# Expert stage of a routed feed-forward layer: row buffers released after the transposes, outputs two tiles to a bank, empty slots skipped in the adds

## The reference

```
x = layernorm(x + power_attention(x))            # 4 x 1024 tokens of 256 values
scores = softmax(x @ gate_w.T)                   # 64 experts
topk_w, topk_idx = top_k(scores, 6)              # 6 experts for each of the 4096 tokens
buf[e, slot] = x[token]                          # 64 x 768 slots; what is over 768 is dropped
g, u = buf @ w_gate[e].T, buf @ w_up[e].T        # 256 -> 176
eo = (silu(g) * u) @ w_down[e].T                 # 176 -> 256
y[token] += eo[e, slot] * weight(token, e)       # scatter-add back to the tokens
x = layernorm(x + y + shared_expert(x))
```

## Time and profile before

| | us |
|---|---|
| median of 3 runs (lowest, highest) | 2573.97 (2572.37, 2574.27) |
| the profiled execution, its own time | 2557.7 |
| its span in the profile | 2555.9 |
| busy in the span: PE / DVE / ACT / POOL | 2312.3 / 1397.8 / 1248.9 / 1578.3 |

### The profile page before, as it was taken

The page is one execution under the profiler, slowest core; times in us unless marked ns, Lnnn a source line. Parts: engine busy times, 40 slices in busy tenths (PEclk is TensorE's granted clock), DMA queues, the critical chain, the costliest instruction groups (busy, mean ns, idle before and its releaser), DMA issues.

```text
span 2555.9 us, 34620 instructions
## 1 busy us (share of the span) xinstructions
PE 2312.3 (90%) x11876; PEld 1793.6 (70%) x11880; DVE 1397.8 (55%) x2813; ACT 1248.9 (49%) x2302; POOL 1578.3 (62%) x1421
## 2 busy tenths in 40 slices
PE   5999999999999899999999999998797999989981
PEld 4777776776767677776667777666685887778871
DVE  2444444445564454557445455745666766656664
ACT  3444444444434344343444443434234777767764
POOL 2566555544578654457855445784074888788885
PEclk8999999999999999999999999999798999999996
DMA  3766741122123112111411211224355999889987
GB/s 125 302 238 261 279 157 63 54 63 64 40 64 119 54 52 87 40 40 69 138 31 53 88 40 38 71 76 146 119 188 163 216 212 202 193 197 213 210 165 230
DMA packets 162663, 329.68 MB, mean 129 GB/s; under 512 B 17552, under 2 KB 98192, under 8 KB 162480
## 3 DMA queue, kind: packets, MB, share of 16 engines
q1 hardware_dynamic: 114144, 262.01, 30.4%
q0 software_dynamic: 48192, 65.04, 14.0%
q10 hardware_dynamic: 144, 0.33, 0.0%
HBM read 172.21 MB, written 155.11 MB: 128 GB/s over the span
## 4 chain that ended last, share of the span: by engine, by line
PE 61%; POOL 10%; DMA 9%; DVE 8%; issue 7%; ACT 5%; POOLq 0%; SPq 0%; ACTq 0%; DVEq 0%
PE bank L686 37%; PE bank L1038 13%; POOL slots L1944 4%; DMA y_part<-y_e,xr 4%; PE bank L696 4%; POOL nacc L1903 3%; PE bank L1048 3%; DMA xr<-slots 3%; POOL y_part L1954 2%; PE bank L1138 2%; PE bank L1035 1%; DVE acc L1563 1%; DMA w_raw_f<-in_wffn,job_w 1%; ACT a L1288 1%; DVE ub L1526 1%
## 5 line engine op out<-in xcount | busy, mean ns | idle before, releaser
L1903 POOL TENSOR_TENSOR nacc<-nacc,a 128x512 f32<-128x512 f32 (+1 forms) x384 | 448.0, 1167 | 286.7 <-ACT a L1292 137.6
L1038 PE MATMUL bank<-a,v 128*128 128x512 f32 x1024 | 529.3, 598 | 0.0
L1954 POOL DMA_INDIRECT y_part<-y_e,xr x256 | 436.5, 1705 | 119.2 <-issue 74.5
L1288 ACT ACTIVATE a<-bank,c_s 128x512 f32<-128x512 f32 x384 | 263.7, 687 | 164.2 <-PE bank L686 148.5
L686 PE MATMUL bank<-q_hi,k_hi 128*128 128x512 f32 (+1 forms) x640 | 324.4, 507 | 12.1 <-DVE ub L1526 6.0
L1292 ACT ACTIVATE a<-ub 128x512 f32<-128x512 f32 (+1 forms) x256 | 133.9, 523 | 394.5 <-DVE ub L1526 382.9
L1903 POOL TENSOR_TENSOR nacc<-a,a 128x512 f32<-128x512 f32 (+1 forms) x128 | 148.9, 1163 | 252.1 <-ACT a L1288 194.6
L1944 POOL DMA_INDIRECT slots<-rows,slot_u x192 | 198.3, 1033 | 163.0 <-DVE slot_u L1689 110.9
L1563 DVE SCALAR_TENSOR_TENSOR acc<-bank,rec,acc 128x256 f32<-128x256 f32 x512 | 223.3, 477 | 98.5 <-PE bank L686 94.5
L686 PE MATMUL bank<-q_lo,k_hi 128*128 128x512 f32 (+1 forms) x640 | 240.0, 375 | 0.0
L686 PE MATMUL bank<-q_hi,k_lo 128*128 128x512 f32 (+1 forms) x640 | 238.3, 372 | 0.0
(11 more groups left out here) (212 smaller groups left out, 5671.6 us busy)
## 6 DMA issues: line engine op xcount, KB each, us to landing
slots<-acc SPq DMA_DIRECT2D x65, 816.0 KB, 7.2
w_raw_f<-in_wffn SPq DMA_DIRECT2D x66, 624.0 KB, 6.7
xr<-slots SPq DMA_DIRECT2D x64, 544.0 KB, 4.6
decay_all<-decay_dram SPq DMA_DIRECT2D x128, 128.0 KB, 3.4
w_hi<-w_dram SPq DMA_DIRECT2D x24, 384.0 KB, 4.7
w_lo<-w_dram SPq DMA_DIRECT2D x24, 384.0 KB, 5.4
sum<-y_part SPq DMA_DIRECT2D x16, 512.0 KB, 10.7
wc_hi<-wc_dram SPq DMA_DIRECT2D x24, 256.0 KB, 3.9
```

The costliest lines, as they stand in the source:

```text
L1038: e.matmul(dst, v[n % 3][:, s, :], a32[u % NA][:, :, :], start=first, stop=False, skip_group_check=True).then_inc(s_av)
L1288: e.activation(squares, score_bank(u)[:, 0:R * w].rearrange("p (r t) -> p r t", r=R), ACT.Square, scale=c_s[b % 2][:, g * (g - 1) + s, h:h ...
L1903: e.tensor_tensor(out_, a, b, op).then_inc(s_nadd)
L1954: e.indirect_dma_start(out=y_part[part], out_offset=bass.IndirectOffsetOnAxis(ap=x_rows[:, j, TOKEN_COL:TOKEN_COL + 1].bitcast(U32), axis= ...
```

## The change

- Rows: `rows_in` waits until the expert four before has been transposed and picked, not for its adds. For that DVE copies the four token numbers of each partition to `row_token` (eight buffers, and four for the over passes), and the adds read them there. XS goes from 5 to 4, YS from 3 to 4.
- Outputs: a `down` task does two tiles, ten matmuls into both halves of one bank; ACT evacuates it in two instructions. The second task's evacuation comes after `hidden` 3.
- Transposes: the three products of `gate_up` become tasks of their own; the transposes of x+1 stand behind the first of them, `pick` behind the transposes.
- Adds: an empty slot now names row 1,048,576 + its position; `y_part` has only the 4096 real rows, and the indirect DMA is told to leave out numbers out of bounds (`oob_is_err=False`). Two fill transfers of the attention stage go (73 become 71).

The diff, cut to its core:

```
-WS, XS, YS, HS, XE, RS = 4, 5, 3, 4, 4, 4
+WS, XS, YS, HS, XE, RS = 4, 4, 4, 4, 4, 4
+KEPT = 8
...
     def turn(x_id):
-        do("pick", x_id)
         for pair in range(tiles_of(x_id) // 2):
             on_spare("turn_x", x_id, pair)
+        do("pick", x_id)
-    def down(x_id):
-        for j in range(tiles_of(x_id)):
-            on_spare("down", x_id, j)
+    def down(x_id, pairs):
+        for pair in pairs:
+            if pair < tiles_of(x_id) // 2:
+                on_spare("down", x_id, pair)
...
+        do("gate_up", k, 0)
+        do("hidden", k, 0)
         if x_id + 1 < E + KJ:
             turn(x_id + 1)
-        do("gate_up", k)
-        do("hidden", k, 0)
         if x_id + 2 < E + KJ:
             do("split_hi", x_id + 2)
+        do("gate_up", k, 1)
         do("hidden", k, 1)
         if x_id + 2 < E + KJ:
             do("split_lo", x_id + 2)
+        do("gate_up", k, 2)
         do("hidden", k, 2)
         if x_id:
-            down(x_id - 1)
+            down(x_id - 1, (0,))
         do("hidden", k, 3)
+        if x_id:
+            down(x_id - 1, (1,))
...
             prev = x_id - XS
             if prev >= 0:
-                once.wait_ge(c_add[prev % 2], added(prev))
+                once.wait_ge(s_spare, spare["turn_x", prev, MT // 2 - 1] + 1)
+                once.wait_ge(c_pick, prev + 1)
...
+                elif x_id >= KEPT:
+                    once.wait_ge(c_add[x_id % 2], added(x_id - KEPT))
+                n = tiles_of(x_id)
+                e.tensor_copy(row_token[kept_at(x_id)][:, 0:n], rows_of(x_id)[:, 0:n, TOKEN_COL].bitcast(U32))
...
-            def add_rows(x_rows, j, y, part, sem):
+            def add_rows(token, j, y, part, sem):
                 e.indirect_dma_start(
-                    out=y_part[part], out_offset=bass.IndirectOffsetOnAxis(
-                        ap=x_rows[:, j, TOKEN_COL:TOKEN_COL + 1].bitcast(U32), axis=0),
-                    in_=y_e[y][:, j, :], in_offset=None, bounds_check=N + CAP - 1, oob_is_err=True,
+                    out=y_part[part], out_offset=bass.IndirectOffsetOnAxis(ap=token, axis=0),
+                    in_=y_e[y][:, j, :], in_offset=None, bounds_check=N - 1, oob_is_err=False,
                     compute_op=ALU.add).then_inc(sem, 16)
...
-            e.iota(slot0[:, :, TOKEN_COL].bitcast(I32), pattern=[[P, CT]], base=N, channel_multiplier=1).then_inc(s_init)
+            e.iota(slot0[:, :, TOKEN_COL].bitcast(I32), pattern=[[P, CT]], base=NOWHERE, channel_multiplier=1).then_inc(s_init)
```

More of the change, by code:

```diff
@@ L342, in shared_up @@
         for half in range(2):
-            do("gate_up", 2 * m + half)
+            for i in range(3):
+                do("gate_up", 2 * m + half, i)
             hidden(2 * m + half)
@@ L465, in build @@
             raw_loads += 1
-    down_of = {x_id: spare["down", x_id, tiles_of(x_id) - 1] for x_id in range(E + KJ)}
+    down_of = {x_id: spare["down", x_id, tiles_of(x_id) // 2 - 1] for x_id in range(E + KJ)}
     shared_down_of = {m: spare["shared_down", m, 1] for m in range(M)}
@@ L1101, in route, with gate_up_part, gate_up @@
                 ins.then_inc(s_spare)
-            def gate_up_passes(k, w, x_hi, x_lo, width):
-                b0 = 3 * (k % 2)
+            def gate_up_part(k, part, w, x_hi, x_lo, width):
+                cols = GU_COLS[part]
                 g_hi, g_lo = gate_up_w(wf_hi[w]), gate_up_w(wf_lo[w])
[L1106 to L1110, removed]
+                product(e, bank[3 * (k % 2) + part][0:cols.stop - cols.start, 0:width], [
+                    (g_hi[:, c, cols], g_lo[:, c, cols], x_hi[:, c, :], x_lo[:, c, :]) for c in range(CC)]).then_inc(c_gu)
+            def gate_up(k, part):
                 w, i = job_of(k)
@@ L1122, in gate_up @@
                 width = MAIN if k < 2 * M + E else OVER
-                gate_up_passes(k, w, xe_hi[i][:, :, 0:width], xe_lo[i][:, :, 0:width], width)
+                gate_up_part(k, part, w, xe_hi[i][:, :, 0:width], xe_lo[i][:, :, 0:width], width)
             def shared_down(m, pair):
@@ L1146, in turn_x, with down @@
                 turn_rows(bank[6 + spare[task] % 2], rows_of(x_id), pair)
-            def down(x_id, j):
-                task = "down", x_id, j
+            def down(x_id, pair):
+                task = "down", x_id, pair
                 k = 2 * M + x_id
+                ps = bank[6 + spare[task] % 2]
                 once.wait_ge(c_hl, 2 * k + 2)
                 once.wait_ge(*out_before(task))
-                down_passes(e, [(k % HS, slot_w(x_id))], j * P, bank[6 + spare[task] % 2][:, 0:C], True).then_inc(s_spare)
+                for jj in range(2):
+                    ins = down_passes(e, [(k % HS, slot_w(x_id))], (2 * pair + jj) * P, ps[:, jj * C:(jj + 1) * C], jj == 0)
+                ins.then_inc(s_spare)
             parts = dict(g_rows=g_rows, g_turn=g_turn, g_sums=g_sums, g_cum=g_cum, col=col, val=val, score=score,
@@ L1171, in over_body @@
                 e.wait_ge(c_h, 2 * (k - 1))
-                gate_up_passes(k, w, xe_hi[0][:, :, 0:OVER], xe_lo[0][:, :, 0:OVER], OVER)
+                for part in range(3):
+                    gate_up_part(k, part, w, xe_hi[0][:, :, 0:OVER], xe_lo[0][:, :, 0:OVER], OVER)
                 e.wait_ge(c_hl, 2 * k + 2)
@@ L1352, in turn_x, with down @@
                              bank[6 + m % 2][:, :].rearrange("p (c t) -> p c t", c=CC), ACT.Copy).then_inc(c_xh)
-            def down(x_id, j):
-                m, y = spare["down", x_id, j], x_id % YS
+            def down(x_id, pair):
+                m, y = spare["down", x_id, pair], x_id % YS
                 once.wait_ge(s_spare, m + 1)
@@ L1358, in down @@
                 y_wait(once, x_id)
-                e.activation(y_e[y][:, j, :], bank[6 + m % 2][:, 0:C], ACT.Copy, scale=row_w_of(x_id)[:, j:j + 1]).then_inc(s_out_of[m % 2])
+                for jj in range(2):
+                    j = 2 * pair + jj
+                    ins = e.activation(y_e[y][:, j, :], bank[6 + m % 2][:, jj * C:(jj + 1) * C], ACT.Copy,
+                                       scale=row_w_of(x_id)[:, j:j + 1])
+                ins.then_inc(s_out_of[m % 2])
             parts = dict(w_split=w_split, wv_split=wv_split, wc_split=wc_split, x_split=x_split, g_turn=g_turn, g_sums=g_sums,
@@ L1994, in down @@
                         once.wait_ge(c_add[part], added(x_id - 2))
-                add_rows(rows_of(x_id), j, x_id % YS, part, c_add[part])
+                for j in (2 * pair, 2 * pair + 1):
+                    add_rows(row_token[kept_at(x_id)][:, j:j + 1], j, x_id % YS, part, c_add[part])
             parts = dict(acc_add=acc_add, em_mask=em_mask, w_rest=w_rest, wv_rest=wv_rest, wc_rest=wc_rest, av=av, route=route, scatter=scatter, over_rows=over_rows,
```

23 lines of the change are left out of this document (12 added, 11 removed).

## The result

| | before | after |
|---|---|---|
| median of 20 runs (lowest, highest) | 2572.21 (2566.74, 2578.99) | 2578.24 (2573.51, 2584.95) |
| ratio, 95% interval | | 1.0026 [1.0017, 1.0034] |
| profiled execution, its own time / span | 2557.7 / 2555.9 | 2579.88 / 2577.9 |

2521 us was forecast, with 2507 to 2563 as the range. The time is 57 us above the forecast and outside the range, on the side of "slower", which had 0.10.

A forecast was written before the change was run, and what follows sets the result against it. Expert passes were held near 8 us by PE with its waits, POOL and the DMA engines, plus stalls; 490.8 − 58 × 7.7 = 44.2, and 9 at the end, made 53 us off: 2521 us, range 2507 to 2563.

The forecast's parts named there:

- The size of the add: POOL's indirect add in the expert passes: leaving out a quarter of its rows shortens it from 1.56 to 1.35 us.
- a ≤ 1.49: The longest add, in us, with which POOL's four adds per expert still fit a pass of 7.7.
- B: Rival: leaving rows out makes no add cheaper to issue, POOL bounds at 7.96 us a pass; 2559 us, chance 0.22.
- The stall as a constant: POOL in each expert pass: one long add waits for DVE's wf_lo, costing 0.52 us.
- Room on POOL: POOL's adds in before: three times 1.86 and one 2.38 make 7.96 us, as much as a pass.
- PE without its waits: PE in the expert pass: waits of 0.18 and 0.23 go, 0.1 is added; 7.98 becomes 7.67 us, taken as 7.7.
- The loop of ACT and DVE: The new order's dependency loop between ACT and DVE in a pass: 7.5 us, under PE's 7.67.
- Rows' buffers: Expert row loads: the wait for adds goes; loads lie four passes, 30 us, ahead against 5.54, so XS 4 costs nothing.
- DMA engines: DMA in the expert pass: the adds' queue falls from 4.05 to 3.0 us, the sum to 6.6, under 7.7.
- The end: Last eight adds, over rows: half-empty adds save 7 us and POOL's lag 2, together 9, between 4 and 14.
- the other rule: DVE's new fp32 SBUF copy may block POOL's descriptor writing, up to 0.18 us for each of 64 copies.

The follow-up runs named there:

- adds_in_range: Changed kernel, but empty slots name rows behind the 4096, so all 128 rows of each add are sent; 2559.86 us, ratio 1.0028 to before.
- in_bank_in_range: Changed kernel with silu(g) * u written back into its PSUM bank and every row of the adds sent; 2515.25 us, ratio 0.9833 to before.
- before_again: The kernel before, unchanged, run again as a yardstick with a second profile; 2555.67 us, ratio 1.0011 to before.
- h_in_bank: Changed kernel with silu(g) * u written back into its PSUM bank, so ha_lo and hb's low part have one SBUF input; 2513.87 us, ratio 0.9846 to before.

## Why the prediction was wrong

- **The size of the add: the step that failed first.** "I take 1.35" stood between 1.17 and the old 1.56, all from the idea that an add is paid by row. It is 1.56 with or without a quarter of its rows (adds_in_range, in_bank_in_range), and with the stalls 1.75 in the mean. The need was written down in the same place: a pass of 7.7 wants a ≤ 1.49. With 1.56 the forecast could not hold, whatever PE did. The rival that says so, B, had 0.22; the median add was measured, a cheaper one was not, and B should have been the forecast.
- **The stall as a constant.** B's own number, 2559, failed too. It took one stall of 0.52 per pass as given, from one pass. The stalls of before are 37 us, 0.6 a pass, but they hang on where the adds and DVE's instructions meet, and the change moves both. After it they are 51 us: adds that end 1.43 us after `ha_lo` cost 24.7, where they cost 0.3 before (1.4 in before_again). That the new order moves `ha_lo`, `hb` and the adds against each other could have been read from the timeline of DVE, had I listed all instructions with two SBUF inputs, and not the one that happened to lie on an add. The mechanism was right and is now tested, its reach was not seen. (The largest share, that of `h_b` and `ha_lo`, a list of instructions with two SBUF inputs would not have foretold in full: most of these adds meet `h_b`, which has one.)
- **Room on POOL.** "7.96: as much as a pass" was right for before, and the 15 us that B gave to the change were 58 × (8.22 − 7.96). But POOL had only 18.8 us of idle time in all, of which 8 come at the stage's start; the change could win 11 of these at most, and did, and lost 14 to stalls.
- **PE without its waits** was right, and a little cautious: 7.43 instead of 7.7. The loop of ACT and DVE, 7.5 by my sum, isn't longer than that.
- **Rows' buffers** was right: the wait is gone, and four passes of lead suffice.
- **DMA engines** was right in direction: 39.2% against the 3.0 / 7.7 = 39% worked out. That it fits to the percent is partly luck, as fewer adds fell into the window; h_in_bank, whose passes are at 7.47, has 45.7%. It bought nothing.
- **The end.** 9 us were to come from over experts' half-empty adds; an empty add costs as much as a full one, so nothing came.
- The rule of the Trainium skill ("SBUF — State Buffer", "Who interferes with whom") that a DVE instruction with two SBUF inputs holds up a GpSimd instruction that reads SBUF agrees with 58 of 58 adds above; it doesn't tell of the 24 on `h_b`. The price put on the other rule, up to 0.18 us for each fp32 copy, isn't there in the trace of after: of the adds without a stall, 56 have a whole copy inside them and 115 touch none, and the median is 1557 ns for both.

## What to carry to other kernels

Before a change to the order, add up the busy time, gaps and idle time of every engine's queue over the stage, and ask what the change takes from the one with the least idle time; if it takes nothing there, the gain of the others turns into waits. When instructions of two engines stall each other, list every pair that can, since an order that is better for one engine can put other pairs on top of each other. Here leaving an intermediate in PSUM, so that two of the three VectorE instructions with both inputs in SBUF had only one there, took 46 us off the changed kernel and 7 off the one before, where the change alone cost 6.

## What the runs showed of the hardware

- An indirect accumulate whose out-of-bounds rows are left out takes as long to issue as a full one: 1561 ns against 1562, with 25% of the rows left out. Its bytes do go (3.49 to 2.63 MB in 50 us), its packets don't (3825 to 3900).
- Such an accumulate is stalled by a VectorE instruction with both inputs in SBUF that began before it and still runs 0.13 us after its start (557 of 558 adds); it then ends 1.43 us after that instruction's end. One that begins after the accumulate's start stalls nothing (0 of 60), so a VectorE instruction of 1.45 us passes unseen between two adds that start 1.86 us apart.
- A VectorE subtraction with one input in PSUM takes nearly as long as with both in SBUF (0.69 us for `ha_lo`, against 0.68), and stalls no add (h_in_bank).
- Open: 24 adds of after are stalled from within `h_b`, until the end of the `ha_lo` behind it, while none is stalled from within `h_a` with `wf_lo` behind it. What distinguishes the two isn't known.
